# A language-model tower on one core: the last pair's experts summed in PSUM with the gates multiplied into the hidden layer, and the expert stage of the pair before it done among the last pair's scores

## The reference

```
# 1. tokens:  t = sin/cos features of the four ids (24 of them)
h  = layernorm(relu(t @ W1 + b1) @ W2 + b2) * gamma + beta + 0.1 * (t @ Wres + bres)      # 64 channels
# 2. attention with 8 heads of 64 channels, one key and one value for all heads, over a layer norm of h
h += Wo(softmax(q k^T / sqrt(8)) v)
# 3. experts over a layer norm x2 of h: 6 experts, the 2 best by the router, softmax of their two weights
rh = relu(x2 @ router_w1 + b);  w = softmax(rh @ router_w2 + b);  top 2
e1 = relu(x2 @ expert_w1 + b1); e2 = relu(e1 @ expert_w2 + b2); y = e2 @ expert_w3 + b3   # for each expert
out = h + sum over the two chosen experts of weight * y
```

## Time and profile before

| what | value |
|---|---|
| median of 3 runs | 659.18 us (656.67 to 659.66) |
| profiled execution, its own time | 659.5 us |
| profiled execution, span | 657.7 us |
| busy PE, VectorE (DVE), ScalarE (ACT), GpSimd (POOL) | 636.6, 522.1, 476.0, 279.1 us |
| mean granted TensorE clock | 0.987 of full |

### The profile page before, as it was taken

How to read it: one execution, slowest core, us unless ns; L and a number is a source line. 1 busy time by engine, 2 the same in 40 slices (tenths; PEclk the granted TensorE clock), 3 DMA queues, 4 the chain that set the end, 5 groups by cost and what they waited for, 6 DMA issues and landing times.

```text
span 657.7 us, 27431 instructions
## 1 busy us (share of the span) xinstructions
PE 636.6 (97%) x11936; PEld 365.8 (56%) x11936; DVE 522.1 (79%) x1030; ACT 476.0 (72%) x1214; POOL 279.1 (42%) x374
## 2 busy tenths in 40 slices
PE   8899998999999999999999999999999999999995
PEld 7344555546655466555655456554665555555563
DVE  5688776878787986979778788879869798778667
ACT  2688885887669766896768876697668967688643
POOL 2342313514654074632935146540746329131184
PEclk7799999999999999999999999999999999999999
DMA  5000000000000000000000000000000000000001
GB/s 179 2 1 2 2 3 3 3 2 3 19 2 2 2 3 19 3 2 2 3 19 2 2 2 19 2 3 2 3 19 2 3 2 3 18 2 2 3 4 34
DMA packets 9864, 6.79 MB, mean 10 GB/s; under 512 B 8720, under 2 KB 9104, under 8 KB 9616
## 3 DMA queue, kind: packets, MB, share of 16 engines
q1 hardware_dynamic: 9456, 4.77, 2.5%
q10 hardware_dynamic: 288, 0.27, 0.1%
HBM read 2.93 MB, written 2.10 MB: 8 GB/s over the span
## 4 chain that ended last, share of the span: by engine, by line
PE 91%; ACT 4%; DVE 3%; issue 1%; POOL 0%; ACTq 0%; DVEq 0%; POOLq 0%
PE s_bank L618 33%; PE s_bank L584 32%; PE s_bank L717 3%; PE s_bank L598 3%; PE s_bank L798 3%; PE s_bank L835 3%; PE s_bank L809 3%; ACT p L916 2%; PE s_bank L872 1%; PE s_bank L695 1%; PE s_bank L729 1%; PE s_bank L647 1%; PE s_bank L629 1%; ACT g L922 1%; DVE nmax L1090 1%
## 5 line engine op out<-in xcount | busy, mean ns | idle before, releaser
L916 ACT ACTIVATE p<-s_bank,nmax 128x512 f32<-128x512 f32 x512 | 347.6, 693 | 132.1 <-DVE nmax L1090 131.9
L1090 DVE TENSOR_REDUCE nmax<-s_bank 128x1 f32<-128x512 f32 x512 | 324.5, 681 | 44.9 <-PE s_bank L584 43.4
L584 PE MATMUL s_bank<-kf,g 64*64 64x512 f32 x2048 | 257.7, 593 | 2.3 <-ACT h1t L951 1.3
L618 PE MATMUL s_bank<-p,woz 64*64 64x256 f32 x4096 | 245.0, 376 | 0.5 <-ACT g L922 0.5
L618 PEld LDWEIGHTS s_bank<-p,woz 64*64 64x64 f32 x4096 | 157.4, 133 | 105.1 <-issue 31.8
L418 POOL TENSOR_TENSOR woz<-cst,rz 128x256 f32<-128x256 f32 x126 | 74.7, 614 | 234.2 <-DVE rz L1096 234.2
L584 PEld LDWEIGHTS s_bank<-kf,g 64*64 64x64 f32 x2048 | 75.9, 133 | 90.1 <-issue 41.2
L916 ACT ACTIVATION_READ_ACCUMULATOR p<-s_bank,nmax 128x1 f32 x512 | 107.1, 209 | 0.0
L1102 DVE STREAM_TRANSPOSE m<-s_bank 128x512 f32<-128x512 f32 x64 | 45.9, 717 | 36.9 <-PE s_bank L618 36.9
L1452 POOL TENSOR_TENSOR st<-st,power 128x8 f32<-128x8 f32 (+3 forms) x25 | 38.8, 1552 | 34.5 <-DVE st L1112 34.5
L427 POOL TENSOR_TENSOR y<-y,gt 128x768 f32<-128x768 f32 x28 | 41.3, 1475 | 2.7 <-DVE y L1361 2.7
(11 more groups left out here) (134 smaller groups left out, 523.8 us busy)
## 6 DMA issues: line engine op xcount, KB each, us to landing
tower_out<-o SPq DMA_DIRECT2D x16, 128.0 KB, 2.8
cst<-consts SPq DMA_DIRECT2D x1, 1102.0 KB, 8.0
e2t<-ids SPq DMA_DIRECT2D x2, 384.0 KB, 5.1
cst<-consts SPq DMA_DIRECT2D x1, 352.0 KB, 5.7
cst<-consts ACTq DMA_DIRECT2D x1, 256.0 KB, 3.6
e2t<-ids SPq DMA_DIRECT2D x1, 192.0 KB, 3.9
cst<-consts SPq DMA_DIRECT2D x1, 128.0 KB, 3.4
e2t<-ids SPq DMA_DIRECT2D x1, 64.0 KB, 2.1
```

Source lines behind the costliest of these rows:

```text
L584: last = pe.matmul(double[half(q), 512 * r:512 * r + 512], g[half(r), a // 2 % 2, a % 2, first:first + 64], kf[half(r), par, a // 4, :], s ...
L618: last = pe.matmul(bank("PV", i, a)[half(q), 512 * hh:512 * hh + 256], woz[half(r), kept, 2 * mm + hh, :], keys[:, q, :, :], start=(part = ...
L916: nc.scalar.activation(p[:, 8 * kept + c % 8, :], bank("S", i, c - r)[:, 512 * r:512 * r + 512], ACT.Exp, bias=nmax[:, c % 16:c % 16 + 1], ...
L1090: nc.vector.tensor_reduce(nmax[:, c % 16:c % 16 + 1], bank("S", i, c - r)[:, 512 * r:512 * r + 512], AX.X, ALU.max, negate=True).then_inc( ...
```

## The change

For pair 7 the gates are multiplied into the hidden layer before the third expert matrix, so that PE sums the experts itself:

- `gated_out` replaces `ffn_out` and `outputs` for L0 and L1. GT: PE spreads each gate over 64 partitions and turns it, by matmuls whose stationary side is one gate column broadcast to 64 columns and whose moving side is the identity (for each couple of experts e and each couple of tiles 8 matmuls of 64 columns). GT_DVE: VectorE multiplies `e2t` by them in place. GB: 4 matmuls of 64 columns for each couple of tiles turn the gates themselves, ScalarE copies them to `gts` (6 partitions of each half), and they multiply the rows of the bias `b3rows`. Y then accumulates the six experts and the bias into one bank OUT, and one VectorE instruction for each unit adds the residual into `o_last`. The bias preload (L824), the gate products of 768 columns, the reductions, and GpSimd's sums are gone for pair 7. Its outputs go out by one store for each unit and sequence.
- The layer norm of L0 and L1 is made with `bn_stats` and `bn_aggr` on VectorE (`moments_of`, `normed`) in place of mean, centring, ScalarE's squares and `rstd`. The power -0.5 stays on GpSimd.
- Table `Z` of pair 6 becomes that of the ordinary pairs, except that ScalarE instead of VectorE empties its E2 banks: all of its pieces lie within slots 1 to 63.
- `L` gets new slots throughout. The tables `A`, `P`, `P0`, `P1`, `F` and the first values' slots are moved.
- 5 more warm matmuls stand between the tokens of sequence 0 and those of sequence 1; before the transpose of L1 there are 3 instead of 12.

```diff
-                  ("e3", NE * C), ("e3b", NE * C), ("lead", C), ("rank", NE), ("b2row", C)):
+                  ("e3", NE * C), ("e3b", NE * C), ("b3rows", C), ("rank", NE), ("b2row", C)):
...
-WARM0, WARM, WARM_T = 9, (1, 4), 12
-
-
-V_FIRST, V_FIRST_ACT = 31, 31
+WARM0, WARM, WARM_T = 9, (1, 5, 4), 3
+
+
+V_FIRST, V_FIRST_ACT = 26, 25
...
 A = {
-    "Q": 11, "RZ": 7, "PV": (13, 15), "MT": 15, "G": 10, "OS": 6}
+    "Q": 11, "RZ": 7, "PV": (13, 15), "MT": 15, "G": 10, "OS": 0}
 
 P = {
-    "H1": 6, "H1_ACT": 6, "TOK": (9, 9, 10), "TOK_DVE": 10, "SQA": 10, "LNA2": 11, "LNB": 28, "SQB": 31,
-    "LNB2": 35, "T": 39, "T_ACT": (39, 39), "V": 41, "V_ACT": (40, 40), "LNA2_POOL": 19, "LNB_POOL": 29,
-    "LNB2_POOL": 31}
+    "H1": 6, "H1_ACT": 5, "TOK": (7, 9, 10), "TOK_DVE": 10, "SQA": 12, "LNA2": 12, "LNB": 27, "SQB": 31,
+    "LNB2": 34, "T": 39, "T_ACT": (39, 39), "V": 41, "V_ACT": (40, 40), "LNA2_POOL": 13, "LNB_POOL": 23,
+    "LNB2_POOL": 27}
 
 P0 = {
-    "SQA": 0, "LNA2": 6, "LNA2_POOL": 0, "LNB": 10, "LNB_POOL": 7, "SQB": 10, "LNB2": 13, "LNB2_POOL": 11,
-    "T": 22, "T_ACT": (21, 23)}
+    "SQA": 7, "LNA2": 9, "LNA2_POOL": 4, "LNB": 13, "LNB_POOL": 6, "SQB": 15, "LNB2": 19, "LNB2_POOL": 9,
+    "T": 23, "T_ACT": (23, 23)}
 
 P1 = {
-    "SQA": 15, "LNA2": 21, "LNA2_POOL": 21, "LNB": 28, "LNB_POOL": 25, "SQB": 37, "LNB2": 47,
-    "LNB2_POOL": 49, "T": 55, "T_ACT": (55, 55), "V": 63, "V_ACT": (63, 63), "TOK_ACT": 11, "H1": 2,
+    "SQA": 26, "LNA2": 37, "LNA2_POOL": 27, "LNB": 45, "LNB_POOL": 39, "SQB": 47, "LNB2": 48,
+    "LNB2_POOL": 44, "T": 55, "T_ACT": (55, 55), "V": 63, "V_ACT": (63, 63), "TOK_ACT": 11, "H1": 2,
     "H1_ACT": 3, "TOK": (8, 9, 10)}
 
 F = {
-    "FIN": (12, 12), "LN": 12, "SQ": 15, "LN2": 21, "T": 30, "T_ACT": 28, "R": 32, "R_ACT": 31, "L": 37,
-    "GATE": (37, 40, 43, 43, 45, 45, 45), "GATE_ACT": (38, 42), "E1": (35, 39, 41), "E1_ACT": (35, 39, 40),
+    "FIN": (12, 12), "LN": 12, "SQ": 15, "LN2": 20, "T": 30, "T_ACT": 29, "R": 32, "R_ACT": 31, "L": 37,
+    "GATE": (37, 39, 39, 42, 44, 45, 45), "GATE_ACT": (37, 42), "E1": (35, 39, 45), "E1_ACT": (33, 39, 45),
     "E2": (40, 48, 52), "E2_DVE": (40, 49, 51), "Y": (54, 58, 63, 63), "Y_DVE": (54, 58, 63, 63),
-    "LN_POOL": 10, "LN2_POOL": 25, "Y_POOL": (61, 61, 63, 63)}
+    "LN_POOL": 1, "LN2_POOL": 16, "Y_POOL": (48, 53, 58, 59)}
 
 Z = {
-    "FIN": (10,), "LN": 10, "SQ": 17, "LN2": 20, "T": 30, "T_ACT": 28, "R": 32, "R_ACT": 31, "L": 40,
-    "GATE": (40, 43, 53, 53, 53, 60, 66), "GATE_ACT": (48, 55), "E1": (34, 55, 67), "E1_ACT": (33, 55, 65),
-    "E2": (45, 68, 68), "Y": (70, 74, 91, 95), "Y_DVE": (70, 76, 91, 103), "LN_POOL": 10, "LN2_POOL": 23,
-    "Y_POOL": (88, 92, 105, 114), "E2_ACT": (44, 68, 69)}
+    "FIN": (12,), "LN": 12, "SQ": 15, "LN2": 20, "T": 30, "T_ACT": 29, "R": 32, "R_ACT": 31, "L": 37,
+    "GATE": (37, 39, 39, 42, 44, 45, 45), "GATE_ACT": (37, 42), "E1": (35, 39, 45), "E1_ACT": (33, 39, 45),
+    "E2": (40, 48, 52), "Y": (54, 58, 63, 63), "Y_DVE": (54, 58, 63, 63), "LN_POOL": 1, "LN2_POOL": 16,
+    "Y_POOL": (48, 53, 58, 59), "E2_ACT": (40, 49, 51)}
 
 LAST_PARTS = ((0, 4, 6), (6, 8))
 
 L = ({
-    "FIN": (61, 65), "LN": 65, "SQ": 66, "LN2": 68, "LN2_POOL": 75, "T": 73, "T_ACT": 74, "R": 91,
-    "R_ACT": 91, "L": 94, "GATE": (95, 98, 98, 103, 118, 124, 125), "GATE_ACT": (97, 127),
-    "E1": (78, 92, 98), "E1_ACT": (80, 94, 104), "E2": (93, 121, 121), "E2_ACT": (95, 118, 125),
-    "YB": (118, 126, 127), "Y": (125, 127, 127), "Y_DVE": (127, 127, 127), "Y_POOL": (119, 89, 123)}, {
-    "FIN": (88,), "LN": 82, "SQ": 83, "LN2": 91, "LN2_POOL": 97, "T": 95, "T_ACT": 97, "R": 103,
-    "R_ACT": 104, "L": 113, "GATE": (113, 115, 115, 115, 117, 117, 117), "GATE_ACT": (111, 122),
-    "E1": (99, 105, 124), "E1_ACT": (111, 111, 126), "E2": (118, 124, 127), "E2_ACT": (118, 126, 127),
-    "YB": (126,), "Y": (127,), "Y_DVE": (127,), "Y_POOL": (119,)},)
+    "FIN": (60, 67), "LN": 68, "LN2": 79, "LN2_POOL": 73, "T": 80, "T_ACT": 97, "R": 89, "R_ACT": 102,
+    "L": 103, "GATE": (105, 105, 108, 108, 110, 111, 114), "GATE_ACT": (110, 112), "E1": (108, 113, 118),
+    "E1_ACT": (106, 111, 114), "E2": (119, 123, 126), "E2_ACT": (116, 116, 121), "Y": (127, 127, 127),
+    "Y_DVE": 126, "GT": (121, 123, 126), "GB": 126, "GT_DVE": (116, 119, 123), "GB_ACT": 123}, {
+    "FIN": (74,), "LN": 92, "LN2": 95, "LN2_POOL": 80, "T": 88, "T_ACT": 102, "R": 103, "R_ACT": 103,
+    "L": 108, "GATE": (107, 117, 118, 122, 123, 124, 126), "GATE_ACT": (112, 123), "E1": (99, 113, 114),
+    "E1_ACT": (103, 111, 112), "E2": (126, 126, 126), "E2_ACT": (124, 126, 126), "Y": (127, 127, 127),
+    "Y_DVE": 127, "GT": (127, 127, 127), "GB": 127, "GT_DVE": (127, 127, 127), "GB_ACT": 127},)
 
...
@@ -752,7 +778,7 @@
                         pe.wait_ge(u.norm.sums, 1)
                         free("XT", u.u)
                         warm(WARM_T, bank("XT", u.u))
-                    pe.wait_ge(u.norm.steps, 3 * u.n + 3)
+                    pe.wait_ge(u.norm.steps, 2 if u.last else 3 * u.n + 3)
                     free("XT", u.u)
                     for t in range(t0 // 2, t1 // 2):
...
+                f, many = u.f, len(u.js)
+                for e in range(EP):
+                    if slot == f["GT"][e]:
+                        if e == 0:
+                            pe.wait_ge(u.gated, 1)
+                        free("GT", u.u, e)
+                        for x in range(2):
+                            for n, j in enumerate(u.js):
+                                for r in range(2):
+                                    for c in range(2):
+                                        first, one = 512 * r + C * (many * x + n), 2 * e + x
+                                        last = pe.matmul(bank("GT", u.u, e)[half(c), first:first + C],
+                                                         gt[half(r), 9, 2 * j + c, one:one + 1].to_broadcast([64, C]),
+                                                         k("ident")[half(r), half(r)], start=True, stop=True,
+                                                         skip_group_check=True)
+                        last.then_inc(u.gt_ps, 1)
+                if slot == f["GB"]:
+                    free("GB", u.u)
+                    for n, j in enumerate(u.js):
+                        for r in range(2):
+                            for c in range(2):
+                                first = 512 * r + C * n
+                                last = pe.matmul(bank("GB", u.u)[64 * c:64 * c + NE, first:first + C],
+                                                 gt[half(r), 9, 2 * j + c, :], k("ident")[half(r), half(r)],
+                                                 start=True, stop=True, skip_group_check=True)
+                    last.then_inc(u.gb_ps, 1)
+                for e in range(EP):
+                    if slot == f["Y"][e]:
+                        if e == 0:
+                            free("OUT", u.u)
+                        pe.wait_ge(u.e2_gated, e + 1)
+                        if e == EP - 1:
+                            pe.wait_ge(u.gb_sb, 1)
+                        for x in (2 * e, 2 * e + 1, NE)[:2 + (e == EP - 1)]:
+                            for n, j in enumerate(u.js):
+                                for c in range(2):
+                                    for q in range(2):
+                                        rows, tokens_of = half(c), slice(128 * j + 64 * q, 128 * j + 64 * q + 64)
+                                        if x == NE:
+                                            rows = slice(64 * c, 64 * c + NE)
+                                            left, right = gts[rows, tokens_of], k("b3rows")[rows, :]
+                                        else:
+                                            left, right = e2t[rows, x, tokens_of], k("e3")[rows, C * x:C * x + C]
+                                        last = pe.matmul(bank("OUT", u.u)[half(q), 512 * c + C * n:512 * c + C * n + C],
+                                                         left, right, start=(x == 0), stop=(x == NE),
+                                                         skip_group_check=True)
+                        if e == EP - 1:
+                            last.then_inc(u.y_ps, 1)
...
@@ -878,6 +946,7 @@
             warm(WARM[0], bank("H1", 1))
             for step in range(1, 4):
                 tokens(0, step)
+            warm(WARM[1], bank("H1", 1))
             tokens(1, 0)
             tokens(1, 1)
...
+                    act.wait_ge(u.gb_ps, 1)
+                    for c in range(2):
+                        rows = slice(64 * c, 64 * c + NE)
+                        by_half = bank("GB", u.u)[rows, :].rearrange("q (r x) -> q r x", r=2)[:, :, 0:C * len(u.js)]
+                        last = nc.scalar.copy(gts[rows, u.cols].rearrange("q (j r p) -> q r j p", r=2, p=64),
+                                              by_half.rearrange("q r (j p) -> q r j p", p=64))
```

(55 more changed lines are left out.)

149 lines of the change are left out of this document (73 added, 76 removed).

## The result

The changed kernel takes 667.72 us (median of 4 runs, 667.22 to 668.24) where the kernel before took 657.92 (4 runs, 656.26 to 659.66): a ratio of 1.0156, 95% interval 1.0122 to 1.0189. The forecast was 657.3, the range 650.5 to 664.5; the result lies 3.2 us above it. The profiled execution took 668.24 us with a span of 666.4, against 659.5 and 657.7.

What follows compares the result with a forecast made beforehand. PE was taken to bound the run except at the start, one wait per body and the tail. 659.5 - 3.2 - 0.4 + 0.4 + 0.35 + 1.0 = 657.65, less 0.3 for the median: 657.3 us, range 650.5 to 664.5.

Steps and rivals of the forecast that it cites:

- The start: Before the first scores: five warm matmuls hold PE's clock up, 3.2 us gained; squares moved in the ramp, 0.4 us less.
- Rival 2: At the start: warm matmuls too few or too early to hold the clock, 3.2 us less gain, 660.5; chance 0.15.
- The bodies: Ordinary pairs: PE's work and the one wait per body for the copy of g stay as they were, sum 0.
- Rival 4, the ring: Seven bodies: changed bank order adds waits or removes the one there, 3.9 us to either side of 657.3; chance 0.10.
- Pair 6 among the scores: Last body: 3.98 us of PE work moves ahead of the last scores, the tail loses as much; 0.4 us added.
- X = S' + 14.0: Tail: L0's norm is ready 14.0 us after the last scores' end, its power queued behind GpSimd's sums of pair 6.
- "Gates at X + 9.8": Tail: L0's gates are done 9.8 us after its norm, with L1's transpose at 2.6 and L0's logits at 5.4.
- Gates to end, 12.0: Tail from L0's gates, 9.8 us after its norm, through both units' output to the last residual at 21.8.
- "what takes their place is as long: +0.35 us": Tail: dropped products, reductions and preload are replaced by equally long work, the end moving from 655.25 to 655.6.
- "The clock, 1.0 us": Tail: PE's idle 3 us before L0's norm can lower the clock, costing 1.0 us (bounds 0 and 8).
- Rival 1: Tail from PE's idle time to the end runs at half clock, +8 in place of +1: 664.3; chance 0.13.
- Rival 3: Tail bounded by its fullest queue, ScalarE's 13.9 us: 17 us after L0's norm instead of 21.8, so 652.5; chance 0.22.

Runs made afterwards that it cites:

- b_z: The kernel before with only pair 6's table `Z` moved to the slots of the ordinary pairs: 668.07 us, ratio 1.0170.
- b_zt: b_tables with pair 6's expert stage moved to the ordinary slots as in b_z: 664.22 us, ratio 1.0142.
- b_zy: b_zt with pair 6's last two Y, their additions and sums moved behind L0's norm: 657.97 us, ratio 1.0024.
- a_pool: The changed kernel with only GpSimd's last two sums of pair 6 moved behind the powers of L0 and L1: 667.65 us, ratio 1.0187.
- a_warm12: The changed kernel with 12 warm matmuls in place of 3 before L1's transpose: 667.99 us, ratio 1.0208.
- a_zl: The changed kernel with the old `Z`, shared pieces of `L` at their old slots, GT and GB behind E2, and 12 warm matmuls: 659.78 us, ratio 1.0040.
- a_fill: The changed kernel with five unused matmuls of 512 columns before L0's transpose and 12 warm ones before L1's: 670.88 us, ratio 1.0237.
- a_y: The changed kernel with pair 6's last two Y, their additions and sums moved behind L0's norm: 666.12 us, ratio 1.0148.
- a_e2dve: The changed kernel with pair 6's E2 banks emptied by VectorE in place of ScalarE: 667.21 us, ratio 1.0172.
- a_t: The changed kernel with L1's transpose, router layer and first expert product moved behind L0's logits: 669.18 us, ratio 1.0195.
- b_warm5: The kernel before with only the five warm matmuls between the tokens of sequences 0 and 1: 655.19 us, ratio 0.9984.
- b_tables: The kernel before with the five warm matmuls and the changed kernel's `A`, `P`, `P0`, `P1`, `F` and first values' slots: 654.04 us, ratio 0.9963.
- b_bn: b_tables with the last pair's norm made by `bn_stats`: 654.14 us, ratio 0.9989.
- a_zl3: a_zl with 3 warm matmuls before L1's transpose in place of 12: 659.87 us, ratio 1.0071.

## Why the prediction was wrong

The kernel's last instruction on an engine was forecast for 655.25 - 3.2 - 0.4 + 0.4 + 0.35 + 1.0 = 653.4 us and came at 664.38, 11.0 later. By the prediction's own terms this is 0.4 at the last scores, 1.7 at L0's norm, 5.5 at its gates and 4.4 behind them, less the 1.0 that was set aside for the clock.

**The start** was right in mechanism and low in size. The clock stayed up, first scores 16.90 (17.8 forecast), and at pair 6's last scores the gain was 6.5 us, not 3.6. The first scores alone give 4.6. But this is a gain against the profiled execution, one of the long ones; against the short executions of the kernel before there is none. Rival 2 didn't occur.

**The bodies** were right: pairs 1 to 6 keep their wait for the copy of g, 0.57 us each (0.67 once). Rival 4, the ring, is out.

**Pair 6 among the scores.** S' is where the last scores end, as 545.86 is where those of pair 6 do. It was forecast for 619.8 + 0.4 - 3.6 = 616.6 and came at 616.99, by two errors that cancel: 2.9 us more at the start, and a body of 77.67 us where the sum makes 69.92 + 3.98 + 0.4 = 74.3. PE's busy time in this body grew by 4.8 us (69.28 to 74.07), with just the 120 records that were forecast, in place of 3.98. "0.4 us for a short wait of PE" was mis-sized: PE's idle time in it grew by 3.0 us (0.64 to 3.60). The waits are 1.52 us at L743 for the copy of g, where the last body before has no such wait (it is 1.5 in b_z, b_zt and b_zy too, so it comes with the moved stage), and 0.88 and 0.54 for ScalarE's copies of E2, with 0.62 at L755 in place of 0.42.

**X = S' + 14.0** was right in mechanism: L0's power directly behind pair 6's last sum. It was S' + 15.7. The sums were not dense: GpSimd waited 3.15 us for pair 6's third Y, whose matmuls stand behind a `turn`, and for its addition. That queues on PE and VectorE, not GpSimd alone, hold L0 up is shown by a_pool against b_zy.

**"Gates at X + 9.8"** measured 15.3. This is the largest miss. PE paused from 631.92 to 634.34 with nothing waited for in the trace, 15 matmuls before the end of FIN. L1's residual, which needs these, came at 634.95, and L1's transpose at X + 5.3 and not X + 2.6. The rest is spread over router and logits with the clock at half; a_warm12 got back 2.0.

**Gates to end, 12.0**, measured 16.4. A second pause of 1.7 us and L1's turns and output at half clock (1.56 us for 48 matmuls in place of 0.93, twice) account for 3.0 of the 4.4. These don't make the stage long: it has 14.3 us in a_zl, without a pause in it and with a clock of 0.92 from 640 to 648 us and 0.86 behind (means), and it is 7.6 in every kernel with the old output.

**The step that failed** is the comparison of the tails, "what takes their place is as long: +0.35 us". It made the tail from S' on 35.8 us, and with the clock 36.8, where the kernel before has 39.4 from 615.83 to 655.25. The tail measured 47.4. The forecast did put the gated output's two chains in a row, but it set their sum against the whole tail of before and let the end stay where it was. It never asked for the stage behind the last gate alone, where the old output takes 7.6 us. The gated output, which was to cost nothing, cost 5.4 to 5.7 us in two pairs of kernels that differ in little else. And L0's late norm, which the sum did have, cost more than the 4 us of PE's work that the tail lost: taking two Y from ahead of it gave back 6.3 us.

"The clock, 1.0 us" had the right sign. Rival 1 named the place and the fall, and its time of 664.3 was nearest, but half clock isn't what was shown to cost the 11 us: warming (a_warm12) shortened the stage by 2.0 us and saved no time, and filling the gap (a_fill) cost more than it gave. The rule of the Trainium skill in "TensorE: Matmul & The Clock Gate" (section "What's actually happening"), that idleness brings half clock back, was borne out: 0.52 from 632 to 640 after PE's gaps. It told the fall, and not that the chain would be long at full clock too. Rival 3, a tail by its fullest queue, was the furthest off.

Three costs were shown, all with the start's edits in: pair 6's stage moved with two Y ahead of L0's norm (654.04 to 664.22, and back to 657.97 without these two), the gated output (654.14 to 659.87, and 657.97 to 663.33), and the order of `L` (659.87 to 663.53). They don't add. With the old tail of pair 7 the move costs 10.2 us, with the new one 4.2 (663.53 to 667.72). Gates, norm and order together cost 9.5 us with the old `Z` (654.04 to 663.53) and 3.5 with the moved one (664.22 to 667.72), where N to G is 4.7 us shorter. That shorter stage is shown; why L0's gates come sooner there was not tested. Not settled is what holds a_y, whose first norm is early.

## What to carry to other kernels

Work taken out of a tail that is a chain of latencies shortens it only if nothing on that chain is queued behind it in its new place: look in every engine's queue at what the moved piece's last instruction stands in front of. Ask of each rewriting of an output which of its steps stand behind the last input to arrive: less busy time on VectorE and GpSimd (516.4 and 274.0 us in place of 522.1 and 279.1) was worse here, since the whole last layer came to stand behind the gates. Cut a tail into stages at events that all versions have; the whole hid here what each stage would have shown. And look at the single runs before a gain in the start is read from a profile: it can be the loss of one kind of execution.

## What the runs showed of the hardware that was not expected

PE pauses in runs of small matmuls with nothing to wait for, at a fixed place in its instruction stream. In the changed kernel it is after 113 of 128 of L755 and after 142 of 144 of L903 (2.42 and 1.74 us). a_pool, whose stores to memory lie elsewhere in time, has it at the same place:

```profile
630.17 1.45 PE L755 MATMUL s_bank<-m,v 32*64 32x64 f32 x113 [1.00 <-DVE m L1179]
633.57 0.37 PE L755 MATMUL s_bank<-m,v 32*64 32x64 f32 x15 [1.95 <-issue]
```

and so have a_e2dve (2.64), a_t (1.95), a_fill (2.22) and a_warm12 (1.95). Two of these add matmuls between the two pauses, and the second pause moves by as many. a_warm12 has 9 more warm matmuls, 18 records, and pauses 20 records before the end of L903 in place of 2; a_fill has 14 more, 28 records, and pauses 30 before it (L907 is its L903):

```profile
656.08 0.57 PE L903 MATMUL s_bank<-cst,e2t 64*64 64x64 f32 x20 [1.39 <-issue]
```

```profile
661.49 0.69 PE L907 MATMUL s_bank<-cst,e2t 64*64 64x64 f32 x30 [1.23 <-issue]
```

The other kernels have pauses at other places, such as one of 1.2 to 1.7 us ahead of the router layer in b_warm5, b_tables, b_bn and a_zl3. In all such time is 1.9 us in the kernel before and 5.3 in the changed one. In the window 628 to 664 us of the changed kernel, 6 fetches of instructions with 0.10 MB in all, some 17 KB each, are on record. The Trainium skill, "Runtime: NRT & Kernel Launch" (section "Instruction fetch mechanics"), says that instructions come in blocks of 16 KiB, at a cost mostly hidden. The size agrees; that a block not yet there makes these pauses fits a place that is counted in instructions, but no run changed the fetch itself, and if so it isn't hidden where 142 matmuls are issued in 2.3 us.

`tensor_scalar` with its two scalars from columns of the moments is held up by GpSimd, as the product of two tiles L1127 was the earlier trace rows: 2.59 us in place of 1.43 for six while GpSimd is in its product and sum (a_y). The Trainium skill, "SBUF — State Buffer" (section "SBUF: two separate sides"), names a pair of ports that VectorE and GpSimd lock for a whole instruction, for VectorE with two inputs from there or in its two-port mode. Which of them applies here no run shows.
